# Half of row 0 moves from the dense pass of the first mixture to the scattered slots

## The reference, cut to what matters

```
x = x + scan(layernorm(x), ...)            # per row, along its tokens
x = x + mixture(layernorm(x), Wr, ..., W1, b1, W2, b2)
x = x + conv(layernorm(x), ...)            # per row, along its tokens
x = x + mixture(layernorm(x), ...)

# mixture: N = 4096 tokens, E = 8, C = N // E = 512
idx  = argmax(softmax(x @ Wr + br))        # one expert for a token
pos  = count of earlier tokens (this one included) with the same expert
keep = pos < C                             # later tokens of a full expert get nothing
out  = keep * gate * (relu(gate * x @ W1[idx] + b1[idx]) @ W2[idx] + b2[idx])
```

## Time and profile before

| what | value |
|---|---|
| median of three runs | 481.70 us |
| profiled execution | 481.37 us, span 479.6 us |
| mean granted TensorE clock | 0.867 of full speed |
| PE busy | 374.3 us (78%) |
| DVE busy | 338.5 us (71%) |
| POOL busy | 285.3 us (59%) |
| ACT busy | 240.1 us (50%) |

### The profile page before, as it was taken

One profiled execution on the slowest core, in us unless ns is written; L12 is line 12 of the kernel. 1 busy time (PEld: TensorE's weight loads), 2 busy tenths in 40 slices (PEclk: granted clock), 3 DMA queues, 4 the chain that ended last, 5 costly groups with the idle time before them and its releaser, 6 DMA issues.

```text
span 479.6 us, 5752 instructions
## 1 busy us (share of the span) xinstructions
PE 374.3 (78%) x1703; PEld 189.8 (40%) x1703; DVE 338.5 (71%) x769; ACT 240.1 (50%) x396; POOL 285.3 (59%) x196
## 2 busy tenths in 40 slices
PE   4998943586887978898679978785999787887792
PEld 3333310321521611434324355454556665444341
DVE  4798899999999999997431556763589745245441
ACT  2687846356556646536333349533787111246440
POOL 2142349899999999980665000278537564426755
PEclk9999976598787696799959999997799986599986
DMA  7114240675100100100212215211202021032201
GB/s 215 27 66 133 66 131 0 200 300 152 42 3 1 40 6 1 38 5 2 90 48 71 73 46 156 73 49 44 78 1 61 30 85 56 28 110 77 83 18 32
DMA packets 28555, 32.85 MB, mean 68 GB/s; under 512 B 5213, under 2 KB 20593, under 8 KB 28524
## 3 DMA queue, kind: packets, MB, share of 16 engines
q1 hardware_dynamic: 24268, 25.40, 17.2%
q0 software_dynamic: 3456, 6.31, 4.3%
q10 hardware_dynamic: 800, 0.78, 0.6%
HBM read 13.97 MB, written 19.38 MB: 70 GB/s over the span
## 4 chain that ended last, share of the span: by engine, by line
PE 27%; DVE 25%; issue 18%; ACT 12%; another core or an unknown queue 9%; POOL 3%; DVEq 3%; ACTq 1%; DMA 1%
DVE states L708 12%; PE ps L1549 3%; PE ps L1538 2%; POOL states L853 2%; PE ps L696 2%; ACT scaled L1318 2%; PE ps L730 2%; PE ps L1270 2%; PE ps L1757 2%; ACT ps L702 1%; PE ps L1254 1%; ACT c_xn L1740 1%; DVE stats L937 1%; DVE c_s L1784 1%
## 5 line engine op out<-in xcount | busy, mean ns | idle before, releaser
L853 POOL TENSOR_TENSOR states<-states,c_rows 128x1024 f32<-128x1024 f32 x60 | 143.6, 2429 | 16.6 <-DVE states L708 16.3
L708 DVE TENSOR_TENSOR_SCAN states<-ps,inp 128x1024 f32<-128x1024 f32 x64 | 140.5, 2259 | 0.2 <-issue 0.2
L702 ACT ACTIVATE ps<-ps,bias_p,scale_p 128x1024 f32<-128x1024 f32 x64 | 75.0, 1177 | 63.7 <-PE ps L696 63.6
L696 PE MATMUL ps<-stack,sel 96*128 96x512 bf16 x128 | 48.8, 475 | 40.7 <-DVE states L708 40.7
L1091 POOL DMA_INDIRECT slots<-x,put x52 | 50.9, 978 | 48.1 <-DVE put L1085 34.4
L1214 POOL DMA_INDIRECT x<-answers,put x24 | 23.7, 986 | 55.6 <-DMA answers<-reply 48.7
L1413 POOL DMA_INDIRECT out<-reply,home x32 | 31.8, 992 | 23.2 <-DVE reply L1390 14.4
L696 PEld LDWEIGHTS ps<-stack,sel 96*128 96x128 bf16 x128 | 9.7, 107 | 76.1 <-DVE states L708 69.9
L1390 DVE SCALAR_TENSOR_TENSOR reply<-ps,rows,kept 128x128 f32<-128x128 f32 x64 | 18.5, 344 | 26.2 <-remote 12.1
L730 PE MATMUL ps<-states,red 128*32 128x512 f32 x256 | 36.2, 672 | 0.2 <-POOL states L853 0.2
L1507 ACT ACTIVATE d_hidden<-ps,b 128x512 f32<-128x512 f32 x24 | 16.4, 686 | 39.7 <-PE ps L1541 18.4
(11 more groups left out here) (198 smaller groups left out, 694.7 us busy)
## 6 DMA issues: line engine op xcount, KB each, us to landing
slots<-zero SPq DMA_DIRECT2D x8, 528.0 KB
rows<-slots SPq DMA_DIRECT2D x16, 264.0 KB
steps<-part SPq DMA_DIRECT2D x4, 768.0 KB, 3.3
stack<-steps SPq DMA_DIRECT2D x12, 256.0 KB, 4.2
answers<-x SPq DMA_DIRECT2D x4, 512.0 KB, 3.2
answers<-reply SPq DMA_DIRECT2D x8, 256.0 KB, 2.6
x<-in_x SPq DMA_DIRECT2D x3, 512.0 KB, 5.4
out<-x SPq DMA_DIRECT2D x3, 512.0 KB
```

The source lines that it names most:

```text
L696: last = pe.matmul(bank(ps, slot(b, u) + q), sel[0:PARTS * QUARTER, (g % QG) * P:(g % QG + 1) * P], stack[:, g // QG, bass.ds(b * SEQ + q ...
L702: act.activation(bank(ps, slot(b, u), 2), bank(ps, slot(b, u), 2), ACT.Exp, scale=m["scale_p"][:, group(u):group(u) + 1], bias=m["bias_p"] ...
L708: dve.tensor_tensor_scan(h[:, u * SEQ:(u + 1) * SEQ], bank(ps, slot(b, u), 2), inp[:, b * SEQ:(b + 1) * SEQ], 0.0, ALU.mult, ALU.add).then ...
L853: eng.tensor_tensor(h[:, u * SEQ:(u + 1) * SEQ], h[:, u * SEQ:(u + 1) * SEQ], c_rows[:, b * SEQ:(b + 1) * SEQ], ALU.mult).then_inc(done, 1)
```

## The change

The dense pass keeps only the first half of row 0, with 8 steps in place of 16. The four tiles of the second half are scattered ahead of row 1 and gathered ahead of row 1. The gather now also waits for the store of row 0. VectorE waits for this gather before the statistics of the second half. The expert part on TensorE is preceded by 30 `keep_clock` products, and those ahead of the transposes of row 0's second half go from 5 to 24. The product that makes the filter's matrix moves ahead of them. ScalarE and VectorE take the first half of row 0 through its taps before they turn to the second half.

```diff
-        return self.put_done[n], 16 * self.sent_tiles(n)
+        return self.put_done[n], 16 * len(self.sent_tiles(n))
...
-        return HT if n == 2 * BATCH - 1 else BT
+        return range(HT, BT) if n == 0 else range(HT) if n == 2 * BATCH - 1 else range(BT)
...
-        for b in range(layer == 0, BATCH):
+        for b in range(BATCH):
             sp.wait_ge(*self.router.scattered(layer * BATCH + b))
...
-        if (b, h) == (1, 0):
+        if (b, h) == (0, 1):
+            pool.wait_ge(m["first_stored"], 16)
             pool.wait_ge(m["stored"][0], 16 * (BATCH - 1))
             pool.wait_ge(self.kept_back, 16 * EXPERTS)
...
     def first_statistics(self, dve, h):
+        if h:
+            dve.wait_ge(self.got[0][1], 16 * HT)
...
-    dense = Dense(plan, ps, m, router, 0, (0, 1), 2, (3, 5), (3, 4), (6, 5), (1, 5))
+    dense = Dense(plan, ps, m, router, 0, (0,), 2, (3,), (3, 4), (6,), (1,))
...
(TensorE)
-        dense.steps(pe, 2, 3)
-        dense.turn_rows(pe, 1)
-        dense.turn_marks(pe, 1)
-        dense.steps(pe, 3, 4)
+        dense.steps(pe, 2, 4)
         router.count(pe, 3)
-        dense.steps(pe, 4, 6)
...
+        dense.steps(pe, 4, 5)
         conv.filter_begin(pe)
-        dense.steps(pe, 6, 9)
+        dense.steps(pe, 5, 7)
         conv.filter_middle(pe)
+        dense.steps(pe, 7, 8)
         dense.turn_back(pe, 0)
-        dense.steps(pe, 9, 12)
         conv.filter_end(pe)
-        dense.steps(pe, 12, 16)
-        dense.turn_back(pe, 1)
         need(pe, router.placed, BATCH)
         need(pe, conv.mlp, 5)
         pe.wait_ge(dense.done, 1 + CREDIT)
-        experts.tensor(pe, 0, dense.done)
+        keep_clock(pe, m, ps, 0, 30)
+        experts.tensor(pe, 0)
...
         pe.wait_ge(conv.u_done, conv.stream(0, 0, 0) + CREDIT)
-        keep_clock(pe, m, ps, 1, 5)
+        need(pe, experts.reply, experts.tiles(EXPERTS - 1))
+        conv.toeplitz_tensor(pe)
+        keep_clock(pe, m, ps, 1, 24)
         conv.transpose_first(pe, 1)
         conv.streams(pe, 0, 1)
-        need(pe, experts.reply, experts.tiles(EXPERTS - 1))
-        conv.toeplitz_tensor(pe)
...
(VectorE)
-        experts.vector(dve, 0, lambda dve: dense.finish(dve, 1, m["first_stored"]))
-
-        conv.first_statistics(dve, 1)
+        experts.vector(dve, 0)
+
         conv.taps(dve, 0, 0)
         conv.first_product(dve, 0)
+        conv.first_statistics(dve, 1)
         conv.taps(dve, 0, 1)
...
(GpSimd)
+        router.scatter(pool, 0)
         router.scatter(pool, 1)
...
+        experts.gather(pool, 0, 1)
         for b in (1, 2):
             experts.gather(pool, b, 0)
             experts.gather(pool, b, 1)
```

More of the change, by code:

```diff
@@ L1089, in scatter @@
         need(pool, self.placed, n + 1)
-        for i in range(self.sent_tiles(n)):
+        for i in self.sent_tiles(n):
             pool.indirect_dma_start(out=m["slots"][n // BATCH], out_offset=bass.IndirectOffsetOnAxis(m["put"][:, b, i:i + 1], 0),
@@ L1436, in __init__ @@
         self.pick, self.minus = m["pick"], m["minus"]
-        self.k, self.s0, self.t0, self.h0 = (2, 2 * EXPERTS, BT, 1) if ahead else (0, 0, 0, 0)
+        self.k, self.s0, self.t0, self.h0 = (1, EXPERTS, HT, 1) if ahead else (0, 0, 0, 0)
         if ahead:
@@ L1896, in _ @@
         experts.sync(sp, 1)
-        need(sp, late.done, 3)
+        need(sp, late.done, 2)
         store_last(sp, m)
@@ L1917, in _ @@
         router.count(pe, 2)
-        dense.steps(pe, 2, 3)
-        dense.turn_rows(pe, 1)
-        dense.turn_marks(pe, 1)
-        dense.steps(pe, 3, 4)
+        dense.steps(pe, 2, 4)
         router.count(pe, 3)
-        dense.steps(pe, 4, 6)
-        pe.wait_ge(dense.marked, 2 + CREDIT)
-        pe.wait_ge(dense.hot_taken, 2 + CREDIT)
+        dense.steps(pe, 4, 5)
+        pe.wait_ge(dense.marked, 1 + CREDIT)
+        pe.wait_ge(dense.hot_taken, 1 + CREDIT)
         conv.filter_begin(pe)
-        dense.steps(pe, 6, 9)
+        dense.steps(pe, 5, 7)
         conv.filter_middle(pe)
+        dense.steps(pe, 7, 8)
         dense.turn_back(pe, 0)
-        dense.steps(pe, 9, 12)
         conv.filter_end(pe)
-        dense.steps(pe, 12, 16)
-        dense.turn_back(pe, 1)
         need(pe, router.placed, BATCH)
@@ L2025, in _ @@
         dense.rectify(act, range(1, 2))
-        dense.normalize(act, 1)
         m["tail"]["take_logits"]()
@@ L2032, in _ @@
         dense.rectify(act, range(3, 4))
-        dense.turn(act, 1)
-        dense.take_masks(act, 1)
         router.row_deviations(act, 3)
         dense.rectify(act, range(4, 5))
-        dense.take_hot(act, 1)
         router.probabilities(act, 3)
         conv.filter_abs(act)
-        dense.rectify(act, range(5, 8))
+        dense.rectify(act, range(5, 6))
         conv.filter_exp(act, 0)
-        dense.rectify(act, range(8, 9))
+        dense.rectify(act, range(6, 8))
         dense.take_sum(act, 0)
-        dense.rectify(act, range(9, 11))
         conv.filter_exp(act, 1)
         conv.filter_decay(act)
-        dense.rectify(act, range(11, 14))
         conv.deviations(act, 0, 0)
-        dense.rectify(act, range(14, 16))
-        dense.take_sum(act, 1)
         experts.scalar(act, 0)
@@ L2054, in _ @@
         conv.take_streams(act, 0, 0)
+        conv.first_tap(act, 0, 0)
+        conv.toeplitz_scalar(act)
         conv.deviations(act, 0, 1)
-        conv.first_tap(act, 0, 0)
         conv.copy(act, 0, (1,))
@@ L2059, in _ @@
         conv.first_tap(act, 0, 1)
-        conv.toeplitz_scalar(act)
         conv.v_copy(act, 0)
```

## The result

The kernel after took 490.26 us (median of six executions; 484.7 to 494.76 but for one of 656.43), the kernel before 483.99 us beside it. The ratio is 1.0145, 95% interval 1.0094 to 1.0196. The forecast was 478.5 us, and its range ended at 486. The profiled execution took 489.7 us with a span of 487.9, 8.3 us more than the 479.6 of before.

A forecast was written before the change was run, and what follows sets the result against it. Dense steps of row 0's second half hold up the experts. Start -11.5, reply to normalizing +8.7, clock +2.2 give -0.6 on row 0's path, -3.1 on row 1's; taken as -3 from 481.4: 478.5 us, range 470 to 486.

The forecast's parts named there:

- Scatter of row 0's half: GpSimd ahead of row 1's scatter: four issues, 5 us, fit into 12.91 us of idle time; cost taken as zero.
- Removed dense work: TensorE ahead of the experts: eight steps and one turn back, 20.1 us, go; the last turn back ends at 258.4.
- Thirty kept-clock products: TensorE between dense pass and experts: 6.6 us from 260.4, so the experts start at 267.0.
- Start of the experts: Experts' first transpose moves from 278.5 to 267.0, -11.5 us; bounds -13.5 and, with one late completion of 6.7 us, -4.8.
- Gather, +8.7 us from last reply to normalizing: Row 0's second half: from last reply to normalizing 11.9 us (294.4 to 306.3) instead of 3.2.
- Clock, +2.2 us: TensorE idles seven us ahead of the half's transposes; they and the streams run at the lower clock, bounds 0 and 3.0.
- Row 1's statistics: VectorE, behind row 0's product: at 318.0 against 321.10, -3.1 us.
- Late completion after the long convolution: Between row 0's long convolution (recorded until 324.72) and gate (331.48): taken as there as before, 6.7 us.
- D: Rival: late completion between 250 and 267 or slower filter network; start moves only about 5 us, 481 to 486; chance 0.12.
- B: Rival: the 6.7 us late completion between row 0's long convolution and gate is gone; 470 to 474 us; chance 0.26.
- C: Rival: lower clock from row 0's second half to its long convolution's end, row 0 +7.1, 488.5 us; chance 0.11.
- own sign of being wrong in its core: Wrong if row 0's second-half product ends later than 319, or if scattering row 0 delays row 1's scatter.

The follow-up runs named there:

- group 1: Kernel after and three variants against the kernel before, on a chip without late completions: before 451.86 us, after 450.77 us, ratio 0.9972.
- fourth kernel: Kernel after plus eight kept-clock products in each of the last four dense steps, chip without late completions: 454.14 us, ratio 1.0068 to before.
- group 2: Kernel after and two kept-clock variants against the kernel before, on a chip with late completions: before 487.94 us, after at ratio 1.0050.
- the 43: Kernel after with 43 rather than 24 kept-clock products ahead of the transposes of row 0's second half, late completions: ratio 1.0179 to before.
- the gather alone: Kernel before with its whole dense pass, plus the gather of row 0's second half, its wait and the changed order: 459.65 us, ratio 1.0179.
- 8, 0 and 0: Kernel after with 8 kept-clock products for the 30, none of the 24, none of the 16, late completions: 482.8 us, ratio 0.9882 to before.
- groups 1 and 4: Runs on two chips without late completions; the second priced fewer kept-clock products: before 453.43 us, after 0.9975, variants 1.0013, 0.9961 and 1.0007.
- second late chip: Kernel after with none of the 30, 24 and 16 kept-clock products, where before took 483.27 us: ratio 0.9918; median 483.34 us.
- group 3: Sixteen kept-clock products ahead of row 0's product transposes removed, late completions, before 487.92 us: from after 1.0000, from before 1.0052 (ratios to before).

## Why the prediction was wrong

**Scatter of row 0's half, taken at nothing: right.** In after GpSimd starts it at 218.38 and row 1's at 226.04, still with 2.64 us idle ahead; the loads are issued at 261.24 against 261.45.

**Removed dense work, -20.1 us of TensorE and the end at 258.4: right in seven profiles of late chips** (258 to 261), wrong in the execution profiled, by 9 us (267.4). This is the step that failed. The prediction counted the remaining steps at 2.24 us each, "at full clock". In the execution profiled, each step that waits for ScalarE's answer lasts 5 us, at a granted clock of 0.50 to 0.98. The trace of the kernel before had 4.39 and 3.78 us in the same stretch (from 243.50 to 251.67), and the prediction read its 2.24 us behind it. (In group 1 the dense pass is over at 249.1, 9 us ahead of the forecast, and the loads, issued at 256.69, set the start.) The bound of -4.8 us for the start took one late completion into account; there were three behind each other and a turn back at the lower clock (two parts of 2.07, not 1.15).

**Thirty kept-clock products, 6.6 us: under-sized.** They took 7.9 to 9.0 us on late chips and 8.32 in group 1, where they begin at the lower clock; 6.63 only behind the filled dense steps of the fourth kernel. They lay on the path whenever the dense pass ended late (269.51 to 277.45; VectorE had the first rows scaled by 274.87). In group 1 they cost nothing.

**Start of the experts, -11.5 (bounds -13.5 and -4.8): -1.2 in the execution profiled**, outside the bounds; -10.6 for after in group 2, -9.6 with the 43, and -10.1 in group 1 (259.94 against 270.00 with the gather alone, since the kernel before has no profile there). Put -1.2 in place of -11.5 in the prediction's own sum, and row 0's product comes 9.7 us later than before; it came 9.1 later.

**Experts, 27.4 us: right** (277.28 to 304.69).

**Gather, +8.7 us from last reply to normalizing: right**, +8.4 (11.6 less 3.2).

**Clock, +2.2 us: right**, since the streams took 1.8 us more (3.78 against 1.98) and the granted clock was at 0.50 there (319 to 322 us); from normalizing to the end of the product it is 11.3 us against 9.4. From last reply to the end of the product it is 22.96 us in after and 12.62 before: +10.3, forecast +10.9. The Trainium skill (TensorE: Matmul & The Clock Gate, "Why this matters for your kernels") advises against idle gaps between bursts of products. The trace agrees on the clock of the streams, and on chips without late completions on the time, by about 0.4%. Where completions are late the runs go the other way: 8, 0 and 0 products gave 0.988.

**Row 1's statistics, -3.1: wrong in the execution profiled**, +6.6 (327.74 against 321.10), because they stand behind the product. In group 2 with the 43, where the start came early, they are 1.5 us earlier (321.43 against 322.91). Two small terms do not follow from the prediction's own figures (four strides of the gather are 5.4 us, not 5.1; the 24 products end at 299.7, not 299.5); nothing hangs on them.

**Late completion after the long convolution, taken as unchanged: wrong, the second step that failed.** In after it comes ahead of the convolution, 6.7 us from the recorded end of the transposes to the copy (329.04 to 335.75 by the semaphore events), and in group 2 a second one of 3.7 us follows behind with the 43 (5.1 in after). From product to gate it was 13.0 us before and 14.3 in after, 19.2 with the 43. Product +9.1 and this +1.3 make the gate's +10.5. In group 2, where the start moved as forecast, it is by these rows this step that keeps the earlier start from becoming a gain.

**Which rival.** D (0.12) named the mechanism, a late completion between 250 and 267, but gave it 5 us and one occurrence, hence 481 to 486. Its sum with the measured sizes is -1.2 + 10.3 + 1.3 = +10.4 at the gate; 2.2 us come back behind it, and the span is 8.3 longer. B had it that the late completion behind the long convolution might vanish. It did in the execution profiled (recorded end 341.90, gate 341.94), but a longer one stood ahead of the convolution; a stretch from product to gate without any was seen only in groups 1 and 4. C was there in part. The sixteen took 5.36 us rather than 3.63 and the long convolution 5.50 rather than 3.42; the latter's 2.1 us are inside the 14.3 from product to gate. It did not decide, since in group 1 the same pause left row 0 a long convolution at the higher clock (3.42 us) and no loss. The prediction's own sign of being wrong in its core, a product that ends later than 319, came true (327.65); scattering row 0 did not delay row 1's scatter.

**What stays open.** Why TensorE's semaphores change up to 8 us after the recorded ends of the products, and whether the product or only its signal is late. That in after and its variants the sixteen products ahead of the transposes decide whether it happens there is shown by rows; that it is their activity rather than the pause that their absence leaves is only argued, and that they alone do it is not so, since the kernel before has them. That late completions alone separate after's 0.997 (groups 1 and 4) from its 1.005 to 1.0145 (the others) is shown by the rows for this stretch, and not tested by switching them off on one chip. The second mixture, which also has them, was not studied.

## What to carry to other kernels

A loop whose every round trips between engines can be shortened only if its round-trip time stays what the profile showed. Where a trace shows unexplained late completions, work out the shortened chain also with one of them per step, as the upper bound: here two profiles of nine came out so, and seven did not. Read the time of a step where the steps that remain will stand, not where they run best. Products that only keep the clock are to be re-priced after each change: they are free while something later holds the engine, and here the kernel with fewer of them measured 0.988 on a late chip, where after measured 1.005 to 1.0145 on others of that kind, and cost about 0.4% on the chips without late completions. (With none of them at all, the second late chip gave 0.9918, and no difference by the medians.) Measure on more than one chip before calling a change of one per cent a gain or a loss.

## What the runs showed of the hardware

The same kernel before took 451.86 and 453.43 us on two chips and 483.27 to 487.94 on the others, some 7% apart. Each chip was measured once, so whether it is the chip or its moment is not shown. From 210 to 234 us TensorE's timelines of after in group 1 and of after without the sixteen in group 3, the same kernel up to there, agree within 0.1 us. The count of row 2 ends in the records at 231.3 in both; in group 3 its semaphore comes at 237.2, 5.9 us later, and three further results arrive within 0.15 us of it, though the recorded ends of the products behind the count lie from 232.6 to 234.8. Results that are done one after another and told at once speak for held back signals rather than slow products; this is argued, not shown. In all eight profiles of groups 1 and 4 no semaphore of TensorE changes more than 0.1 us after the recorded end. Nothing that the profile shows at that moment explains it: the granted clock is 1.00 from 231 to 234 on both, and the DMA engines move 200 and 205 GB/s. Three executions on late chips took 656, 1621 and 1776 us; none of them was profiled, and nothing here explains them.
